# A fused decoder layer on one core: the order of scores, a key rope, a high part and the last products in cross attention

## What is computed

```python
x = x + attn(layernorm(x))                  # 128 heads, latent projections, rope part of 64
x = x + xattn(layernorm(x), ctx, ctx, pos)  # cross attention, below
x = x + ffn(layernorm(x))                   # base matrix + 8 low-rank experts, top 2 by a gate
```

```python
q = (query @ Wq) -> 32 heads of 16;  k, v = (ctx @ Wk), (ctx @ Wv) -> 8 heads of 16
q = q * cos + rotate_half(q) * sin;  k = k * cos + rotate_half(k) * sin
probs = softmax(q k^T / 4)           # each k, v head serves 4 q heads
out = (probs v) @ Wo
# ffn
result = x @ base_w.T + base_b + 2 * sum over the two chosen experts of w_e * (x A_e^T) B_e^T
```

## Time and profile before

| | |
|---|---|
| median of 3 runs | 822.26 us (821.90 to 823.88) |
| profiled execution | 821.84 us, its span 820.1 us |
| granted TensorE clock | 1.00 of full speed |
| TensorE busy | 787.5 us, 96% of the span |
| VectorE, ScalarE, GpSimd busy | 630.9, 582.7, 592.5 us |
| begin of unit 0 to end of span | 645.6 to 820.1 us |

### The profile page before, as it was taken

How to read it: one execution, slowest core, us unless ns; L and a number is a source line. 1 busy time by engine, 2 the same in 40 slices (tenths; PEclk the granted TensorE clock), 3 DMA queues, 4 the chain that set the end, 5 groups by cost and what they waited for, 6 DMA issues and landing times.

```text
span 820.1 us, 17892 instructions
## 1 busy us (share of the span) xinstructions
PE 787.5 (96%) x5641; PEld 389.1 (47%) x5641; DVE 630.9 (77%) x1190; ACT 582.7 (71%) x1070; POOL 592.5 (72%) x537
## 2 busy tenths in 40 slices
PE   4999999999999999999999999999999888999997
PEld 3464444444444444444444444444444444555443
DVE  7767676676677788777688877679877789888876
ACT  8757777777777777777777777778776566656651
POOL 7967999999988788888888888879656634222111
PEclk9999999999999999999999999999999999999999
DMA  8355355533434333344333344352322000000001
GB/s 335 112 197 147 90 152 152 168 93 89 105 103 123 92 80 87 96 116 111 103 80 93 88 112 105 102 155 65 83 63 54 29 3 2 12 5 15 19 24 39
DMA packets 52176, 75.80 MB, mean 92 GB/s; under 512 B 10256, under 2 KB 34096, under 8 KB 51616
## 3 DMA queue, kind: packets, MB, share of 16 engines
q1 hardware_dynamic: 52128, 75.23, 33.0%
HBM read 38.69 MB, written 19.40 MB: 71 GB/s over the span
## 4 chain that ended last, share of the span: by engine, by line
PE 85%; DVE 8%; issue 2%; ACT 2%; SPq 1%; DMA 1%; POOL 0%; DVEq 0%; ACTq 0%
PE PS L1570 40%; PE PS L1644 7%; PE PS L1611 7%; PE PS L1645 7%; PE PS L1507 6%; PE PS L1659 5%; PE PS L1745 2%; DVE xm L1311 2%; PE PS L1684 1%; PE PS L1843 1%; PE PS L1621 1%; PE PS L1693 1%; PE PS L1809 1%; PE PS L1860 1%; PE PS L1752 1%
## 5 line engine op out<-in xcount | busy, mean ns | idle before, releaser
L1570 PE MATMUL PS<-XTh,W 128*128 128x512 f16 x1024 | 345.9, 379 | 0.0
L654 POOL TENSOR_TENSOR Pl<-PR,Ph 128x512 f16<-128x512 f32 x254 | 285.8, 1156 | 28.1 <-ACT Ph L936 28.0
L929 ACT ACTIVATE PR<-PS 128x512 f32<-128x512 f32 x256 | 152.8, 597 | 130.9 <-PE PS L1645 124.2
L1125 DVE TENSOR_REDUCE mneg<-PS 128x4 f16<-128x512 f32 x256 | 171.5, 685 | 34.7 <-PE PS L1611 32.9
L1570 PE MATMUL PS<-XTl,W 128*128 128x512 f16 x512 | 193.6, 378 | 0.0
L1113 DVE SCALAR_TENSOR_TENSOR QS<-PS,QC 64x512 f16<-64x512 f32 x256 | 175.5, 685 | 20.3 <-ACT QC L846 16.1
L846 ACT ACTIVATE QC<-PS 64x512 f16<-64x512 f32 x256 | 150.7, 589 | 6.5 <-PE PS L1570 1.6
L1570 PEld LDWEIGHTS PS<-XTh,W 128*128 128x128 f16 x1024 | 96.6, 97 | 119.1 <-issue 25.9
L936 ACT ACTIVATE Ph<-PR 128x512 f16<-128x512 f32 x256 | 139.3, 617 | 0.0
L1611 PEld LDWEIGHTS PS<-KC,QC 112*128 112x128 f16 x1024 | 78.4, 97 | 63.4 <-DVE mneg L1125 2.8
L1611 PE MATMUL PS<-KC,QC 112*128 112x128 f16 x1024 | 99.4, 219 | 0.8 <-ACT QC L846 0.7
(11 more groups left out here) (236 smaller groups left out, 1030.8 us busy)
## 6 DMA issues: line engine op xcount, KB each, us to landing
Wraw<-in_wqr SPq DMA_DIRECT2D x32, 512.0 KB, 4.8
QS<-QC SPq DMA_DIRECT2D x64, 256.0 KB, 3.3
head_outputs<-OS SPq DMA_DIRECT2D x256, 40.0 KB
q_content_parts<-stg SPq DMA_DIRECT2D x12, 256.0 KB, 2.7
k_content_parts<-stg SPq DMA_DIRECT2D x12, 256.0 KB, 3.2
QC<-q_content_parts SPq DMA_DIRECT2D x116, 24.0 KB
KC<-k_content_parts SPq DMA_DIRECT2D x29, 96.0 KB
xs<-in_x SPq DMA_DIRECT2D x8, 256.0 KB, 4.5
```

What stands on the lines that cost most here:

```text
L654: nc.gpsimd.tensor_tensor(Pl[:, 4 * j.s + b], PR[:, b], Ph[:, 4 * j.s + b], ALU.subtract).then_inc(s_pl, 1)
L929: nc.scalar.activation(PR[:, b, :], PS[:, bB[b % 2], :], ACT.Exp, scale=ATT_SCALE).then_inc(s_e, 1)
L1125: nc.vector.tensor_reduce(mneg[:, j.p, j.s, :, b], PS[:, bA[b % 2], :].rearrange("p (j k) -> p j k", j=GH), AX.X, ALU.max, negate=True).th ...
L1570: last = mm(PS[:, bQ[c], :], wt[:, j.w, k, c * P:(c + 1) * P], xt[:, k, sl], start=(i == 0), stop=(i == 3 * KT - 1))
```

## The change

All edits are in lists of instructions or in the numbers that place them. No instruction is added or removed: each engine has as many as before, TensorE, VectorE and ScalarE in another order, GpSimd and SP in the same.

```diff
-        SUMS_AT = {0: 4, 2: 5, 9: 6, 13: 7}
+        SUMS_AT = {0: 4, 5: 5, 8: 6, 13: 7}
...
                 x_exps(u, 0)
+                if u == 8:
+                    norm_high(2, 0, bF[0], s_f)
                 x_out(u - 1)
                 x_exps(u, 1)
-                if u == 8:
-                    norm_high(2, 0, bF[0], s_f)
...
                 if half:
                     dve.wait_ge(s_kvr, 1)
-                    dve.wait_ge(s_xqa, 3)
+                    dve.wait_ge(s_xqa, 2)
...
-                        if v >= 3:
+                        if v >= 2:
                             dve.wait_ge(s_kvr, 2)
...
-                if u == 5:
+                if u == 2:
                     k_rope(1)
...
+            SCORES_FIRST = (1, 4, 5, NU - 5)
...
                 if r == 2 and 0 <= b - 2 < B:
                     gate(b - 2, bF[1], (1, 2))
+                    x_scores(u)
                     outputs_turn(b - 1, bF[0])
...
+                if u in SCORES_FIRST:
+                    x_scores(u)
                 if 0 <= u + 2 < NU:
                     x_rough(u + 2)
...
-                if 0 <= u < NU:
+                if 0 <= u < NU and u not in SCORES_FIRST and not (r == 2 and 0 <= b - 2 < B):
                     x_scores(u)
...
+            base(B - 3, 1)
+            x_back(NU - 2)
             low_turn(B - 3)
-            x_back(NU - 2)
             x_weigh(NU - 1)
-            base(B - 3, 1)
+            base(B - 3, 2)
             x_back(NU - 1)
             norm_turn(2, B - 2, bF[0])
             outputs_turn(B - 1, bT7)
             gate(B - 2, bG)
             project_outputs(B - 1, bP7)
-            base(B - 3, 2)
             lora(B - 3)
             base(B - 2, 0)
+            base(B - 2, 1)
             norm_turn(2, B - 1, bF[0])
-            base(B - 2, 1)
+            base(B - 2, 2)
             low_turn(B - 2)
             pe.wait_ge(s_ge, B - 1)
             gate(B - 1, bG)
-            base(B - 2, 2)
             lora(B - 2)
```

## The result

The changed kernel takes 816.61 us (median of 4 runs, 815.87 to 816.71), the kernel before 822.83 us beside it (4 runs, 821.90 to 823.88): a ratio of 0.9916, 95% interval 0.9903 to 0.9930. It is 6.2 us faster. The prediction said 4.1 us faster, 818.1, and its range ended at 816.7: the direction and the places were right, the size was too small, and the result lies 0.1 us under the range.

A forecast was written before the change was run, and what follows sets the result against it. TensorE, busy 96% of the span, was taken as the bound, with only its gaps to win. Terms 2.1 + 1.28 + 0.8, less 0.05, gave 4.1 us: 818.1 us on the median, range 816.7 to 820.4.

The forecast's parts named there:

- part 3: Second key rope to unit 2, sums of rows 5 and 6 and high part moved: 2.1 us early up to unit 11.
- part 2: Exact scores ahead of rough scores in units 1, 4, 5, 27: unit 2 begins 0.2 us later, unit 27 costs 0.05.
- the price of the scores: Exact scores take some 0.33 of TensorE's queue; moved into the gap, what follows comes 0.32 us earlier.
- Part 1: Exact scores ahead of the outputs' turn in units 9 to 29, once in four: 0.32 us each in four units, 1.28 together.
- rival (b): Maxima's DMA comes late: gain shrinks, sign turns at 0.76 us extra, 824.7 us at 1.1 extra; chance 0.05.
- The margin that I gave the DMA: Unit 17: the maxima row arrives 2.57 us after the copy starts, leaving 0.28 us behind the scores before the outputs' turn.
- rival (a): Rope and moved sums meet GpSimd's operations and slow down: 819.8 to 820.8 us, middle 820.2; chance 0.17.
- Part 4: Tail: a group of four products covers the wait before the weighted low rows; last products come 0.8 us earlier.
- Rival (c): Order changes but nothing moves in the steady part, VectorE sets the pace, parts 3 and 4 remain: 819.4 us; chance 0.14.

The follow-up runs named there:

- the last kernel: Changed kernel plus early output division, weighed values turned back before the gate, scores behind the outputs' turn, early scores in r = 0 and 3: 814.69 us.
- part 1 alone: Kernel before with only the exact scores of units 9, 13, 17, 21, 25, 29 ahead of the outputs' turn: 820.85 us against 823.07.
- the two experiments: Kernel before with only rope and sums moved, 819.71 us; kernel before with GpSimd's last weight split moved from unit 9 to 6, 825.20 us.
- the kernel of the split in unit 6: Kernel before with GpSimd's last weight split moved from unit 9 to unit 6: 825.20 us against 823.06, ratio 1.0029.
- the kernel with the early division: Changed kernel with VectorE's output division between the two row maxima ahead of an outputs' turn: 815.16 us, ratio 0.9903 to the kernel before.

## Why the prediction came out too small

All numbers here are counted from the first turn, so that they can be set against the terms of the sum.

Three steps failed. Largest is part 3 behind unit 9, where I took 0.3 off for slower rows and the rows became faster. Next is the sign of part 2 (0.2 late predicted, 0.3 early measured), then the price of the scores, 0.32 in place of 0.42 per unit.

**Part 1, the scores' price (1.28 predicted, 1.70 measured).** The waits and the units were right: units 17, 21, 25 and 29 gain, unit 13 gains nothing in the end, and the DMA has landed in time (rival (b) is out: 2.54 to 2.59 us wherever the scores wait for it, but for one row of the last kernel, 2.67). The step that failed is the price "taking some 0.33 of TensorE's queue": I read it as the distance from the scores to the weighing. What their removal is worth is the distance between their neighbours with and without them, and that is 0.48 from the turn of maxima to the weighing before against 0.01 after, less the 0.04 that the weighing then takes longer to the next turn (0.61 in place of 0.57). The outputs' turn is not delayed: it stands 0.99 behind the gate's last product in both. Measured 0.41 to 0.45 per unit, four times 0.1 more than predicted. The margin that I gave the DMA was right: in units 13, 17, 21, 25 and 29 the scores start 2.52 to 2.57 us after the copy, as it is due, and 0.22 to 0.27 us of the gap is left behind them (0.28 predicted). (1.70 is the four units of the whole change, 1.74 those of part 1 alone.)

**Part 2 (0.2 late predicted, 0.3 early measured).** The step that failed is "push the rough scores and the turn of the maxima 0.22 us back". The push was there, but only 0.11, since the scores take 0.23 of the queue in front of the rough scores, not 0.33. And I didn't count what the unit saves where the scores no longer stand, 0.43. The two give the 0.32 measured. I had looked at the front of the unit and not at its end. Unit 27 costs and gives nothing: in it the scores now wait 0.75 for the DMA, where the rough scores waited 0.76, and TensorE waits 0.20 for VectorE's low rows (L1351) before the next turn.

**Part 3 up to unit 8 (unit 8 1.5 early predicted, 2.24 measured).** The rope was right: 0.69, 0.75 and 0.69 us, three units earlier, absorbed there, and no wait of the query product in unit 7. Rope and sums alone bring 1.96. Within the prediction's figure of 1.5 stood 0.4 of lateness from units 3 to 6 (0.2 of it part 2's) that didn't come: with part 2's sign wrong, unit 7 begins 0.29 early. That is 0.69 of the 0.74 by which this part was too small.

**Part 3 in units 9 to 11 (2.2 then 2.1 predicted, 2.99 at unit 10 and 3.72 at unit 12 measured; 0.09 of it goes in unit 16, which leaves 3.63).** The prediction added 0.4 for the high part, 0.32 for the scores of unit 9 and 0.2 for the sum in VectorE's waits, and took 0.3 off. The high part alone brought 0.44, the scores of unit 9 nothing (0.38, lost at unit 11), and the sum's new place 0.35. So the 0.32 should not have been in this sum; it hid a part of the miss. The step that failed most is "It won't quite ... I take 0.3 off". The sums' products stayed at 0.29 in their new places, and rival (a) did not come. That was luck of the position: both products begin just ahead of a GpSimd operation (672.11 with L799 at 672.19, 686.29 with L827 at 686.31), and no run shows what they take when they begin inside one. On the other side the slow norm rows, which I had named as the reason for caution, became fast, because VectorE reached them 0.7 us nearer to the end of GpSimd's operation (0.18 before it, not 0.89). That is worth 0.64. With 0.44 and 0.35 it makes the 1.43 that the changed kernel gains from unit 9 to unit 12; in the two experiments it was 0.99 (0.64 and 0.35) and 0.70. The trace of before had both forms (0.55 in the median, 1.18 at most), and I never asked which one the new positions would meet.

The Trainium skill (SBUF, "Who interferes with whom") says that VectorE shares a pair of ports with GpSimd when it reads two SBUF inputs, as the rope does, or works in a mode that takes both ports for one tensor, which a tensor_scalar like the norm rows can enter, and that in such a mode whoever issues first has the pair for its whole instruction. The rope agrees: in the kernel of the split in unit 6 all three of its rows are lengthened, to 1.53, 2.55 and 1.52. The norm rows agree in kind and not in size: if they waited for all that is left of GpSimd's operation, 0.89 and 0.18, they would take some 1.43 and 0.72 (an estimate, the rest plus 0.54), where the rows show 1.18 and 0.54. The measurement decides.

What the traces show instead is this: where norm rows begin inside a GpSimd operation, they end 0.27 to 0.29 us after its end, or take 0.54, whichever is more. With 0.89 left they take 1.18, with 0.44 0.73 (the kernel with early scores in more units), with 0.41 0.70, with 0.32 0.59, with 0.18 0.54. So a shift of 0.7 us can take a whole wait away, as here, or bring one.

**Part 4 (0.8 predicted, 0.81 measured)** was right in the group of 0.86. The 0.05 taken off it was right by luck: I expected it in front of the last norm turn, where nothing is lost (12.15 against 12.16); it comes behind it, where the two low-rank products (L1752) now follow the gate directly and take 0.91 to the next group in place of 0.86. Why was not tried.

**The sum.** 4.13 predicted. To it come 0.42 (part 1), 0.74 (up to unit 8: 2.24 in place of 1.5), 0.79 (from there to unit 17: 1.39 in place of 2.1 - 1.5 = 0.6) and 0.11 (no cost in unit 27, 0.05 in steps of 0.01 or 0.02 in the steady part, 0.01 in the tail): 6.19, as measured. Rival (c), a steady part that doesn't move, is out: from unit 17 on, each group of four units is 0.42 to 0.45 shorter.

The range's lower end fell with it. The bounds of part 1 ended at 1.5 and those of part 3 at 2.4, 2.1 + 0.3 for rows that keep their durations; none allowed a row on the path to become shorter, though the earlier trace rows held one that could.

## What to carry to other kernels

What a short group costs an in-order queue is the distance between the starts of its neighbours with it and without it, at both places, the one that it leaves too; its own length gave 0.32 where 0.42 was moved, and the wrong sign in unit 1. Where two engines hinder each other, work out for every slow row on the path at which phase of the other engine's operation it will begin after the shift, and let the range hold the gain as well as the loss. When a moved group has closed a gap, look at what the neighbouring engines then wait for: here an earlier division and a few more moves of the same kind brought another 2.5 us.

## What the runs showed of the hardware

- The turn of maxima followed directly by the weighing starts 0.01 us ahead of it; with the scores between them the distances are 0.15 and 0.32 to 0.33, and scores followed by rough scores take 0.23, as do rough scores followed by scores. The 0.01 is the same in the changed kernel and in the one with all scores behind the rough scores. Why it depends on the neighbour was not tried.
- Norm rows of 128x512 float32 took 1.18 us when they began 0.14 after the start of a GpSimd operation of 1.03 us, and 0.54 when they began 0.18 before its end; in between they end 0.27 to 0.29 after GpSimd's operation does. A rope of three VectorE rows took 2.1 us with GpSimd idle and 5.6 us beside its splitting.
- The two small DMAs of the maxima took 2.54 to 2.59 us from the start of the copy to the first product wherever that product waited for them, in all kernels, with one row of 2.67.
- The first 640 us, the same in all kernels, ended within 2.2 us of each other from one execution to the next (638.88 in the kernel with rope and sums alone, 639.04 before, 639.91 after, 641.12 in the kernel with the early division), while the 170 us behind them repeat to 0.02 in two executions of the changed kernel. A difference of 1 us between two spans is therefore not to be put down to an edit before the common start is taken off. What makes the start wander stays open.
